# Cross-attention with a routed feed-forward: the third subtraction of the maximum on GpSimd, transpose of the maximum, `places` and `scatter` at later points

## What is computed

```python
x = x + attention(ctx, ctx, layernorm(x))        # softmax(q k^T / sqrt(512)) v, then Wo, bo
g = layernorm(x) @ w_router                       # 4096 x 16
top_k_probs, ei = top_k(softmax(g), 2)
pos = cumsum(one_hot(ei)) * one_hot(ei)           # place of each token within its expert
x = x + collect(expert_ffn(dispatch(x, ei, pos)), ei, pos, top_k_probs)
```

## Time and profile before

| | us |
|---|---|
| median of 3 runs | 1821.96 |
| lowest, highest | 1820.82, 1825.42 |
| profiled execution, its own time | 1826.18 |
| its span from first to last instruction | 1824.5 |

### The profile page before, as it was taken

The page is one execution under the profiler, slowest core; times in us unless marked ns, Lnnn a source line. Parts: engine busy times, 40 slices in busy tenths (PEclk is TensorE's granted clock), DMA queues, the critical chain, the costliest instruction groups (busy, mean ns, idle before and its releaser), DMA issues. The chain is left out here.

```text
span 1824.5 us, 40730 instructions
## 1 busy us (share of the span) xinstructions
PE 1620.5 (89%) x15565; PEld 1057.9 (58%) x15565; DVE 1253.2 (69%) x2427; ACT 602.0 (33%) x902; POOL 735.4 (40%) x708
## 2 busy tenths in 40 slices
PE   8999989999988999989999889999899459999974
PEld 4444856667766667756677666677566125455530
DVE  4443368788778787787887787877878455555524
ACT  2343332333322332333333223323333024454530
POOL 1100143454433454334544334543345254656640
PEclk9999999999999999999999999999999669999985
DMA  4310113222222222222222222222321257989969
GB/s 150 88 47 6 54 42 65 52 46 46 59 64 56 52 46 46 69 58 57 47 46 59 64 57 51 46 46 68 58 52 31 46 158 188 203 217 219 199 84 369
DMA packets 339922, 155.75 MB, mean 85 GB/s; under 512 B 268642, under 2 KB 285026, under 8 KB 339876
## 3 DMA queue, kind: packets, MB, share of 16 engines
q1 hardware_dynamic: 317424, 111.05, 25.2%
q0 software_dynamic: 16896, 35.42, 10.1%
q10 hardware_dynamic: 5556, 8.66, 1.3%
HBM read 95.04 MB, written 60.06 MB: 85 GB/s over the span
## 5 line engine op out<-in xcount | busy, mean ns | idle before, releaser
L45 PE MATMUL sc<-qt,kT 128*128 128x128 f16 x3100 | 520.8, 219 | 3.4 <-POOL before L821 3.4
L46 PE MATMUL sc<-qt,kT 128*128 128x128 f16 x3100 | 520.9, 219 | 0.0
L47 PE MATMUL sc<-qt,kT 128*128 128x128 f16 x3100 | 520.8, 219 | 0.0
L45 PE MATMUL acc<-vv,pT 128*128 128x512 f16 x800 | 316.6, 396 | 15.2 <-DVE pT L1024 7.8
L47 PE MATMUL acc<-vv,pT 128*128 128x512 f16 x800 | 316.0, 395 | 0.0
L46 PE MATMUL acc<-vv,pT 128*128 128x512 f16 x800 | 315.4, 394 | 0.0
L45 PEld LDWEIGHTS sc<-qt,kT 128*128 128x128 f16 x3100 | 303.3, 98 | 8.8 <-POOL before L821 3.9
L46 PEld LDWEIGHTS sc<-qt,kT 128*128 128x128 f16 x3100 | 303.3, 98 | 2.2
L47 PEld LDWEIGHTS sc<-qt,kT 128*128 128x128 f16 x3100 | 303.3, 98 | 0.0
L858 POOL TENSOR_TENSOR sum<-s_T 128x512 f32<-128x512 f32 x32 | 72.8, 2274 | 400.5 <-ACT s_T L909 400.5
L858 POOL TENSOR_TENSOR sum<-sum,s_T 128x512 f32<-128x512 f32 (+1 forms) x160 | 208.7, 1305 | 31.9 <-issue 17.4
(11 more groups left out here) (292 smaller groups left out, 2891.6 us busy)
## 6 DMA issues: line engine op xcount, KB each, us to landing
xq<-in_x_dram SPq DMA_DIRECT2D x32, 256.0 KB, 2.9
x_in<-in_x_dram SPq DMA_DIRECT2D x32, 256.0 KB, 2.8
raw_g<-in_L_ffn_w_gate_dram SPq DMA_DIRECT2D x16, 512.0 KB
raw_f<-in_L_ffn_w_fc_dram SPq DMA_DIRECT2D x16, 512.0 KB
raw_p<-in_L_ffn_w_proj_dram SPq DMA_DIRECT2D x16, 512.0 KB, 3.6
y_dram<-x SPq DMA_DIRECT2D x32, 256.0 KB, 2.9
rows_dram<-row SPq DMA_DIRECT2D x32, 256.0 KB, 2.0
blocks_r<-row_bl SPq DMA_DIRECT2D x32, 256.0 KB, 2.0
```

The costliest lines, as they stand in the source:

```text
L45: pe.matmul(out, s_hi, m_hi, start=first, stop=False)
L46: pe.matmul(out, s_hi, m_lo, start=False, stop=False)
L47: return pe.matmul(out, s_lo, m_hi, start=False, stop=last)
```

## The change

- The subtraction of `m_b` from the third group (tiles 16 to 24, 1152 elements a partition) goes from VectorE's `shift` to GpSimd, as the first instruction of `sums`, with a semaphore of its own, `sub_pool`. The exponential of that group waits for it.
- VectorE's `place` moves from between the second and third `low` to behind the first maximum of the next step; it then serves tile `t-2`. The `low` of group 2 follows directly on that of group 1.
- GpSimd's `scatter` serves tile `t-2` too and moves from the end of the step to behind `add_bias`, ahead of `deviation_q` and `sums`.
- On TensorE, `greatest` goes from block 3 to block 8, `spread` from 6 to 10, `logits` from 12 (18 in the last step) to 16, and `places` from block 23 to behind the first score chunk of the next step.
- In step 1 nothing is placed; at the end `place` and `scatter` of the last two tiles follow one another.

```diff
@@ -691,7 +691,7 @@
         sc_cp = sem("sc_cp")
         rm_rdy, mx_pe, dg_rdy, mb_pe, mb_rdy = sem("rm_rdy"), sem("mx_pe"), sem("dg_rdy"), sem("mb_pe"), sem("mb_rdy")
         st_rdy, pt_rdy = sem("st_rdy"), sem("pt_rdy")
-        sub_rdy, ex_rdy = sem("sub_rdy"), sem("ex_rdy")
+        sub_rdy, sub_pool, ex_rdy = sem("sub_rdy"), sem("sub_pool"), sem("ex_rdy")
         p_hi, p_lo = sem("p_hi"), sem("p_lo")
         pv_part = sem("pv_part")
         sum_rdy, rs_pe = sem("sum_rdy"), sem("rs_pe")
@@ -851,6 +851,10 @@
 
                 def sums(t, h):
 
+                    a, b = groups[NG - 1]
+                    pool.wait_ge(mb_rdy, t + 1)
+                    pool.tensor_tensor(s_T[h][:, a:b, :], s_T[h][:, a:b, :], m_b[:].unsqueeze(1).to_broadcast([P, b - a, P]),
+                                       ALU.subtract).then_inc(sub_pool, 1)
                     for c in range(1, NCH):
                         a, b = chunk[c]
                         pool.wait_ge(ex_rdy, NG * t + group_of(a) + 1)
@@ -862,27 +866,28 @@
                     wait_for(pool, rs_pe, t)
                     pool.tensor_tensor(sum1[:], sum4[:, 0, :], sum4[:, 1, :], ALU.add).then_inc(sum_rdy, 1)
 
-                def step(t, h, post, more, more_q):
+                def step(t, h, post, more, more_q, placed=True):
                     if post:
                         deviation(t - 1)
                         add_bias(t)
+                    if post and placed:
+                        scatter(t - 2)
                     if more_q:
                         deviation_q(t + 2)
                     if more:
                         sums(t + 1, 1 - h)
-                    if post:
-                        scatter(t - 1)
 
                 add_bias(0)
                 sums(0, 0)
                 step(0, 0, False, True, True)
-                step(1, 1, True, True, True)
+                step(1, 1, True, True, True, False)
                 with pool.Fori(1, NT // 2 - 1) as m:
                     for h in range(2):
                         step(2 * m + h, h, True, True, True)
                 step(NT - 2, 0, True, True, False)
                 step(NT - 1, 1, True, False, False)
                 deviation(NT - 1)
+                scatter(NT - 2)
                 scatter(NT - 1)
                 pool.wait_ge(scat, 32 * NT)
 
@@ -905,7 +910,10 @@
 
                 def exponentials(t, h, g):
                     a, b = groups[g]
-                    act.wait_ge(sub_rdy, NG * t + g + 1)
+                    if g == NG - 1:
+                        act.wait_ge(sub_pool, t + 1)
+                    else:
+                        act.wait_ge(sub_rdy, (NG - 1) * t + g + 1)
                     act.activation(s_T[h][:, a:b, :], s_T[h][:, a:b, :], ACT.Exp, bias=e_bias[:],
                                    scale=SM / (XN_S * CTX_S)).then_inc(ex_rdy, 1)
 
@@ -1014,7 +1022,7 @@
                     dve.wait_ge(mb_pe, t + 1)
                     dve.tensor_copy(m_b[:], ps_y[:, 0:P]).then_inc(mb_rdy, 1)
                     dve.drain()
-                    for g, (a, b) in enumerate(groups):
+                    for a, b in groups[:NG - 1]:
                         dve.tensor_tensor(s_T[h][:, a:b, :], s_T[h][:, a:b, :], m_b[:].unsqueeze(1).to_broadcast([P, b - a, P]),
                                           ALU.subtract).then_inc(sub_rdy, 1)
 
@@ -1139,11 +1147,13 @@
                         dve.scalar_tensor_tensor(out=q16[:, D:2 * D], in0=xqs[:], scalar=XN_S, in1=q16[:, 0:D],
                                                  op0=ALU.mult, op1=ALU.subtract).then_inc(q_lo, 1)
 
-                def step(t, h, post, more, more_q):
+                def step(t, h, post, more, more_q, placed=True):
                     if post:
                         residual(t - 1)
                     for c in range(NCH if more else 0):
                         maximum(t + 1, 1 - h, c)
+                        if c == 1 and post and placed:
+                            place(t - 2)
                         if c == 2 and post:
                             normed(t - 1)
                             rows_low(t - 1)
@@ -1161,13 +1172,8 @@
                         shift(t + 1, 1 - h, more_q)
                     if post:
                         route(t - 1)
-                    if more:
-                        low(t + 1, 1 - h, 0)
-                        low(t + 1, 1 - h, 1)
-                    if post:
-                        place(t - 1)
-                    if more:
-                        low(t + 1, 1 - h, 2)
+                    for g in range(NG if more else 0):
+                        low(t + 1, 1 - h, g)
 
                 dve.wait_ge(wr_hi, 1)
                 dve.scalar_tensor_tensor(out=w_r16[:, :, 1, :], in0=w_r[:], scalar=W_S, in1=w_r16[:, :, 0, :],
@@ -1185,12 +1191,13 @@
                 shift(1, 1, True)
                 for g in range(NG):
                     low(1, 1, g)
-                step(1, 1, True, True, True)
+                step(1, 1, True, True, True, False)
                 with dve.Fori(1, NT // 2 - 1) as m:
                     for h in range(2):
                         step(2 * m + h, h, True, True, True)
                 step(NT - 2, 0, True, True, False)
                 step(NT - 1, 1, True, False, False)
+                place(NT - 2)
                 residual(NT - 1)
                 normed(NT - 1)
                 rows_low(NT - 1)
@@ -1257,13 +1264,13 @@
                             last.then_inc(pv_part, 1)
                         if k == 0:
                             row_sum(t)
-                        if more and k == 3:
+                        if more and k == 8:
                             greatest(t + 1)
-                        if more and k == 6:
+                        if more and k == 10:
                             spread(t + 1)
-                        if post and k == (12 if more else 18):
+                        if post and k == 16:
                             logits(t - 1)
-                        if post and k == (23 if more else NK - 1):
+                        if post and not more and k == NK - 1:
                             places(t - 1)
 
                 def logits(t):
@@ -1285,11 +1292,15 @@
                     pe.matmul(ps_m[:, 0:2 * E], ones_b[:], acc_oh[:].rearrange("p k e -> p (k e)"),
                               start=False, stop=True).then_inc(pos_pe, 1)
 
-                def step(t, post, more):
+                def step(t, post, more, placed=True):
                     for c in range(NCH if more else 0):
                         scores(t + 1, c)
+                        if c == 0 and placed:
+                            places(t - 2)
                     if more:
                         tail_scores(t + 1)
+                    else:
+                        places(t - 2)
                     times_values(t, post, more)
 
                 pe.wait_ge(a_const, 13)
@@ -1306,7 +1317,7 @@
                 tail_scores(1)
                 pe.wait_ge(wr_lo, 1)
                 times_values(0, False, True)
-                step(1, True, True)
+                step(1, True, True, False)
                 with pe.Fori(2, NT - 2) as t:
                     step(t, True, True)
                 step(NT - 2, True, True)
```

## The result

The change makes the kernel slower by half a per cent: median 1833.16 us (1831.53 to 1834.29, four runs) against 1822.64 us (four runs), a ratio of 1.0056 with a 95% interval of 1.0038 to 1.0073. The prediction said 1864 us with a range from 1812 to 1895. The direction is right, the size four times too large: 10.5 us instead of 42. The profiled execution took 1831.53 us, with a span of 1829.8; it lies only 5.3 us above the profiled execution of the kernel before (1826.18 us).

A forecast was written before the change was run, and what follows sets the result against it. VectorE's chain was taken to set the lap, with TensorE waiting. A, B and C of 20.0 + 3.3 + 16.8 made 40.1 us against 38.68, +42 us over thirty laps: 1864 us, range 1812 to 1895.

The forecast's parts named there:

- What bounds the kernel: Attention stage: VectorE's chain sets the lap of 38.68 us; TensorE, with 34.3 us of work, waits for it.
- A: VectorE's stretch from `residual` to the end of the folded maximum; forecast 20.0 us a lap, from 18.10.
- C: VectorE's stretch from the broadcast maximum's copy into `m_b` to the next `residual`; forecast 16.8 us, from 16.79.
- Part 1: Third subtraction to GpSimd: its 2.6 us stops VectorE's two, which end after 5.0 us instead of 3.63; +1.35 us.
- side-by-side rival: The engines do not exclude each other for the subtraction: 1.28 us saved, -1.2 us a lap, 1786 us; chance 0.10.
- Part 2: `place` moved between VectorE's first and second maximum: -2.17 us where it stood, +1.9 us where it goes.
- The lower end of 0.65: Moved `place` fully covers the copy's wait and the bias addition's stall, so A grows by only 0.65 us.
- the upper end: Every contention around the moved `place` counts, including a first maximum delayed by the power; A grows by up to 2.35 us.
- Part 3: GpSimd's scatter one tile later and earlier in its order: cost 0, up to 1 us if it stops VectorE twice.
- Part 4: TensorE's transpose, broadcast, logits and `places` moved: B averages 3.3 us instead of 3.79, ends 2.88 and 4.2.
- B: VectorE's stretch from the folded maximum's end to the broadcast maximum's copy into `m_b`; forecast 3.3 us, from 3.79.
- The sum: Whole lap: 20.0 + 3.3 + 16.8 = 40.1 us against 38.68, +1.4 us a lap, +42 us in thirty laps.

The follow-up runs named there:

- e3_pe_only: The kernel before with only TensorE's transpose, broadcast and logits moved to blocks 8, 10 and 16, `places` still at block 23; 1821.5 us, ratio 0.9969.
- e4_no_sub: The changed kernel with the third subtraction back on VectorE; 1790.1 us, ratio 0.9825 to the kernel before.
- the last kernel above: The same run as e10_combined, the faster candidate built from the parts that pay; 1765.5 us.
- e1_sub_only: The kernel before with only the third subtraction given to GpSimd; 1890.3 us, ratio 1.0377.
- e5_early: The changed kernel with the transpose back at block 3 and the broadcast at 6; 1889.6 us, ratio 1.0358 to the kernel before.
- e2_place_only: The changed kernel with the subtraction back on VectorE, transpose at block 3, broadcast at 6, logits at 12; 1811.9 us, ratio 0.9954 to the kernel before.
- the second profile: A repeat profile of an unchanged kernel: 1824.34 us for the kernel before, 1833.29 us for the changed kernel.
- the second pair: The repeat profiles of the kernel before and the changed kernel, both unaltered; 9.0 us apart.
- e8_xb_late: e4_no_sub with GpSimd's bias addition behind the query's power and SyncE's load of the next x behind the row blocks; 1790.4 us, ratio 0.9814.
- the three filled kernels: Unused extra TensorE products ahead of the transpose: eight in e4_no_sub (1779.6 us), twelve in the changed kernel (1825.9 us), thirteen in the kernel before (1806.3 us).
- e10_combined: e4_no_sub with bias addition after the query's scaling, five unused products, blocks 8 and 10 from step 1 (3 and 6 in step 0); 1765.5 us, ratio 0.9683.

## Why the prediction was right and wrong

**What bounds the kernel: right.** VectorE's lap sets the time. The sum A + C follows what stands in VectorE's order in every run (within 0.13 us in e3_pe_only, where TensorE comes late), and TensorE has a stop in each lap.

**Part 1, GpSimd's subtraction: right, slightly too dear.** The 2.6 us for 1152 elements, taken from two rows, was 2.62, and it ran before VectorE's first, one of the two cases that the text named. VectorE's subtractions end at 4.82 instead of the forecast 5.0 us; +1.19 instead of +1.35. With the choice that waits for the first sum the whole part is 1.47 us, where the text had 1.65. The side-by-side rival is refuted by the row of 4.82 us and by e4_no_sub.

**Part 2, `place`: the failing step.** Stretch C was well forecast (-0.16 measured, 0 forecast). In A the text took +1.9 us for the moved `place`, and +1.09 came; this alone is 24 of the 31 us by which the prediction was too high. The mechanism, a two-input operation of `place` stopped by the bias addition, was right; the term was mis-sized in two pieces of its working.

First, "now it can start ahead of that maximum and delay it by some 0.45 us": the power did start ahead, by 0.11 us, and delayed nothing. So the first maximum ends at 4.54 us of the lap and not at 5.02. The bias addition too starts earlier; 0.5 of its 1.42 us pass beside the end of the first maximum, the reciprocal and the pause behind it, and the stop in `place` is 0.75 us and ends at 5.7 us of the lap instead of 6.2. Second, "then some 1.75 us more, then the second maximum": it was 1.44, from 616.78 to 618.22. The old length of 2.17 us, from which the text worked, held two short stalls of its own. Timeline of VectorE in the kernel before, the two operations (in the last kernel above, where nothing stops them, they take 0.16 and 0.15 us):

```profile
681.66 0.36 DVE L1105 TENSOR_TENSOR P<-e_two,P 128x1 f32 x1 [0.17 <-issue]
...
682.19 0.42 DVE L1111 SCALAR_TENSOR_TENSOR ia<-r,off 128x2 f32<-128x2 f32 x1
```

The lower end of 0.65 was nearer to the truth than the value chosen (0.44 off instead of 0.81); I had gone close to the end at which every contention counts. The pieces named for the upper end, 0.65, 1.13 and 0.45, add up to 2.23 and not to the 2.35 of the text.

**Part 3, scatter: right in the lap, wrong at the start.** In the lap it cost nothing; `rstd_q` was ready in time. What I did not look at is the start-up, a term put at nothing. There VectorE's first `query` waits for `rstd_q` behind the first tile's sums, and GpSimd's subtraction stands ahead of those. In the changed kernel the wait is 6.53 us, against 3.71 before (second line):

```profile
237.56 0.21 DVE L1142 TENSOR_SCALAR shift_q<-mv_q,rstd_q 128x1 f32<-128x1 f32 x1 [6.53 <-POOL rstd_q L850]
...
234.40 0.21 DVE L1134 TENSOR_SCALAR shift_q<-mv_q,rstd_q 128x1 f32<-128x1 f32 x1 [3.71 <-POOL rstd_q L850]
```

The start-up loss is 4.2 us in the changed kernel, 3.4 with the subtraction and early blocks (e1_sub_only, e5_early), and none in e2_place_only and e4_no_sub, where `scatter` has moved too. So it comes with the subtraction and not with `scatter`.

**Part 4, TensorE's order: right in kind, too small.** B went to 3.01 (2.94 in the second profile) instead of 3.3, from 3.84 (3.65). It fell for two reasons. Its least value is 2.53 instead of 2.88, with the broadcast two blocks behind the transpose and not three; the text had kept 2.88. And the part above the least value is 0.48 us on average instead of 0.96. This is not because the clock falls more rarely: in the first profiles it falls in 18 of the 28 laps of the changed kernel and in 19 of the kernel before, in the second in 16 and 16. What differs is where in the lap. B in such laps is 3.27 us in the changed kernel, 0.74 above its least, and 4.30 in the kernel before, 1.42 above; it never went over 3.85. The text had this, a fall that is "nearly through" when the broadcast comes, and sized it too small. The stop before the transpose is 2.5 us and not 4, because the lap grew less than I thought. The move of `places` the text priced at nothing; e3_pe_only shows that without it the stop goes there and the gain of the later blocks is not seen.

**The sum.** Forecast +1.4 us a lap. Measured +0.1 (+0.2 in the second pair): A 0.8 less, B 0.3 less, C 0.2 less. Two forces of similar size stand against each other, +0.93 a lap in A and C and -0.7 to -0.8 in B. I had the first too large and the second too small, so their difference came out many times too large. That the direction was right owes something to luck: the steady laps add only 2 us (6 in the second pair), and the 4.2 us of start-up, for which the sum had no term, weigh about as much. The lower end of C in the text, 16.4 (neither stall), is a slip: 16.79 + 1.35 - 2.17 is 16.0; with it the lower ends add up to 37.6 us a lap and not 38.0.

## What to carry to other kernels

Giving GpSimd a part of an elementwise job of VectorE need not shorten VectorE's chain, where both read two tensors from SBUF and exclude each other: here 1.28 us taken off became 1.47 us put on, and the version without it is 43 us faster. When TensorE must wait, find out what that does to its clock: here stops of 2.5 to 4.9 us a lap put up to 2.2 us more on the path, and some work without use in their place was worth 1% on the kernel before. A change made of several moves has to be priced in its combinations: the later blocks alone gave nothing clear, with the later `places` 22 us, and 56 beside the subtraction; the subtraction alone cost 68 us, beside the rest 43.

## What was not expected of the hardware

- A one-element power on GpSimd that starts 0.11 us ahead of a two-input instruction of VectorE does not delay it (0.69 us, its usual length), while a 512-element addition stops VectorE until it ends. Where the power starts in the same hundredth of a microsecond as such a maximum, it is the power that is held: 1.11 us instead of 0.55. The Trainium skill, "SBUF — State Buffer", section "Who interferes with whom", has the pair held for the whole instruction by whoever starts first; for the power the measurement says less than that, as far as GpSimd's starts and ends in a profile are exact.
- By and large, the more TensorE stands idle in a lap, the more laps have a fall of the granted clock. Idle us between its matmuls in a lap and laps with a fall, of 28: 4.9 and 27 (e1_sub_only), 4.2 and 28 (e5_early), 3.3 and 19 (before), 3.3 and 18 (changed), 2.9 and 20 (e3_pe_only), 2.9 and 15 (e2_place_only), 2.6 and 13 (e8_xb_late), 2.5 and 15 (e4_no_sub); with 0.6 to 1.3 us (the three filled kernels and e10_combined) there is none.
- The two profiles of the kernel before, and the two of the changed one, differ in the lap by B alone. With TensorE's order moved alone, the executions of one kernel spread from 1806.6 us at a granted clock of 0.954 to 1834.8 at 0.935.
